# The router of batch 5 moved one or two places forward in the last batch of an attention loop

## The reference

```
# attention, per batch
q, k, v = x @ Wq.T, x @ Wk.T, x @ Wv.T
attn = softmax(q k / sqrt(D) + bias)
x = layernorm(x + (attn v) @ Wo.T)
# router
scores = sigmoid(xf @ gate_w.T)                  # [T, 32]
group_scores = scores.reshape(-1, 8, 4).max(-1)  # 8 groups
keep the 4 best groups; idx = top 6 experts of these
w = scores[idx] / sum * 2.5
# experts
y = sum over e of w[e] * (silu(xf @ w11[e].T) * (xf @ w33[e].T)) @ w22[e].T
shared = silu(xf @ sw1.T) * (xf @ sw3.T) @ sw2.T
x = layernorm(x + y + shared)
```

## Time and profile before

| | us |
|---|---|
| median of 3 runs | 552.78 |
| the three runs | 549.53, 552.78, 555.93 |
| the profiled execution | 551.69 |
| its span | 549.9 |
| PE busy | 463.3 (84%) |
| DVE busy | 367.0 (67%) |
| ACT busy | 320.9 (58%) |
| POOL busy | 226.6 (41%) |

### The profile page before, as it was taken

One profiled execution on the slowest core, in us unless ns is written; L12 is line 12 of the kernel. 1 busy time (PEld: TensorE's weight loads), 2 busy tenths in 40 slices (PEclk: granted clock), 3 DMA queues, 4 the chain that ended last, 5 costly groups with the idle time before them and its releaser, 6 DMA issues.

```text
span 549.9 us, 12959 instructions
## 1 busy us (share of the span) xinstructions
PE 463.3 (84%) x3218; PEld 385.7 (70%) x3219; DVE 367.0 (67%) x1711; ACT 320.9 (58%) x1087; POOL 226.6 (41%) x244
## 2 busy tenths in 40 slices
PE   4368878768878777879896999999999999999993
PEld 3245657556756555754356899999999999998772
DVE  4025586929696989787734677777777777771574
ACT  1049898848888898954103556555565555653024
POOL 0000000070435353737771557666666666665000
PEclk9757999979898999899998999999999999999998
DMA  4579749976959682439966855555555555521994
GB/s 133 120 232 253 176 113 259 238 225 202 237 138 237 179 202 71 142 95 401 413 233 188 307 160 166 151 156 167 147 166 151 165 165 165 153 73 66 421 414 171
DMA packets 68715, 107.92 MB, mean 196 GB/s; under 512 B 9269, under 2 KB 55098, under 8 KB 67520
## 3 DMA queue, kind: packets, MB, share of 16 engines
q1 hardware_dynamic: 53472, 74.62, 47.6%
q0 software_dynamic: 10752, 26.13, 14.3%
q10 hardware_dynamic: 4448, 6.65, 3.6%
HBM read 64.03 MB, written 43.33 MB: 195 GB/s over the span
## 4 chain that ended last, share of the span: by engine, by line
PE 45%; DMA 20%; DVE 10%; SPq 8%; POOL 6%; issue 6%; ACT 4%; POOLq 0%; ACTq 0%; DVEq 0%
PE bank L726 20%; PE bank L735 10%; POOL routed L1437 6%; DMA k_scratch<-k_lo 6%; DMA expert_w<-expert_out 6%; PE bank L716 5%; DVE s_neg L1015 4%; DMA k_pack<-k_scratch 4%; SPq L431 3%; ACT probs L831 2%; PE bank L500 2%; DMA xt<-xT 2%; SPq L382 2%; DMA xg_all<-routed 2%; PE bank L563 1%
## 5 line engine op out<-in xcount | busy, mean ns | idle before, releaser
L1437 POOL DMA_INDIRECT routed<-rows,position x96 | 93.5, 974 | 192.4 <-DVE position L1179 164.0
L1447 POOL DMA_INDIRECT expert_out<-rows,out_row x128 | 130.5, 1020 | 84.1 <-issue 61.2
L831 ACT ACTIVATE probs<-s_neg,m_neg 128x128 f32<-128x128 f32 (+1 forms) x256 | 113.9, 448 | 41.6 <-DVE m_neg L1015 41.4
L1015 DVE CUSTOM_DVE_ANT_0 s_neg<-bank,bias_sb 128x128 f32<-128x128 f32 (+1 forms) x256 | 79.8, 351 | 56.5 <-PE bank L532 55.3
L929 ACT ACTIVATE eg<-bank 128x128 f32<-128x128 f32 x128 | 35.5, 277 | 84.5 <-PE bank L726 82.5
L735 PE MATMUL bank<-expert_w,ea 128*128 x256 | 78.6, 389 | 2.2 <-issue 1.0
L532 PE MATMUL bank<-k_pack,q_pack 128*128 128x256 f32 (+1 forms) x128 | 59.3, 472 | 15.8 <-DMA k_pack<-k_scratch 13.2
L726 PEld LDWEIGHTS bank<-x1T,xn 128*128 128x128 f32 x512 | 67.9, 194 | 3.5 <-issue 0.3
L726 PE MATMUL bank<-x1T,xn 128*128 128x128 f32 x512 | 68.5, 277 | 0.0
L936 ACT ACTIVATE rows<-bank,pick 128x256 f32<-128x256 f32 x128 | 60.0, 468 | 2.6 <-DVE out_row L1346 2.2
L546 PE MATMUL bank<-cst,probs 128*128 128x128 f32 x256 | 44.2, 300 | 13.8 <-ACT probs L831 12.9
(11 more groups left out here) (162 smaller groups left out, 798.8 us busy)
## 6 DMA issues: line engine op xcount, KB each, us to landing
xg_all<-routed SPq DMA_DIRECT2D x128, 137.5 KB, 2.2
expert_w<-expert_out SPq DMA_DIRECT2D x16, 768.0 KB, 13.1
expert_w<-expert_weights SPq DMA_DIRECT2D x9, 1024.0 KB, 23.8
q_pack<-q_scratch SPq DMA_DIRECT2D x32, 256.0 KB, 4.7
routed<-empty SPq DMA_DIRECT2D x8, 550.0 KB, 13.5
k_pack<-k_scratch SPq DMA_DIRECT2D x16, 256.0 KB, 7.0
expert_w<-expert_weights ACTq DMA_DIRECT2D x8, 384.0 KB, 4.9
xt<-xT SPq DMA_DIRECT2D x9, 256.0 KB, 7.1
```

The costliest lines, as they stand in the source:

```text
L831: act.activation(probs[g % 2][qb][:, 2 * pair + r, :], s_neg[u][:, r, 0:n], ACT.Exp, bias=m_neg[:, u, r:r + 1], scale=-1.0, accum_out=row_ ...
L1015: dve.tensor_tensor_reduce(out=s_neg[u][:, r, 0:n], in0=SCORES[u][:, n * r:n * r + n], in1=bias_sb[:, REP * g + 2 * pair + r, SEQ - n:SEQ] ...
L1437: pool.indirect_dma_start(routed, bass.IndirectOffsetOnAxis(ap=position[b % ROW_BUFS][:, t, j:j + 1], axis=0), rows[b % ROW_BUFS][:, t, :] ...
L1447: pool.indirect_dma_start(expert_out, bass.IndirectOffsetOnAxis(ap=out_row[:, k:k + 1], axis=0), ey[k], None, bounds_check=TOKENS * TOPK - ...
```

## The change

In the last batch of the loop (`ahead` is false there and only there) the pieces of the router of batch 5 have a table of their own, `LAST_AT_UNIT`. Pieces 0, 1 and 2 keep their units, pieces 3 to 11 stand in an earlier unit than before. `ranks` of batch 5 stands on PE after unit (2, 1) instead of (3, 0).

```
-                        if g == 3 and u == 0 and two_behind:
+                        if (g, u) == ((3, 0) if ahead else (2, 1)) and two_behind:
                             ranks(b - 2, par)
...
             AT_UNIT = {(0, 1): (0,), (0, 2): (1,), (0, 3): (2,), (1, 1): (3,), (1, 2): (4, 5),
                        (1, 3): (6,), (2, 0): (7, 8), (2, 2): (9,), (3, 1): (10,), (3, 2): (11,)}
+            LAST_AT_UNIT = {(0, 1): (0,), (0, 2): (1,), (0, 3): (2, 3), (1, 1): (4, 5), (1, 2): (6,),
+                            (1, 3): (7, 8), (2, 0): (9,), (2, 2): (10,), (2, 3): (11,)}
...
-                            for piece in AT_UNIT.get((g, u), ()):
+                            for piece in (AT_UNIT if ahead else LAST_AT_UNIT).get((g, u), ()):
                                 router_piece(b - 2, par, piece)
```

## The result

The changed kernel takes 546.51 us (median of 16 runs, 541.82 to 551.98), the kernel before 549.0 us (median of 16 runs, 545.63 to 555.93). The ratio is 0.9939, with a 95% interval from 0.991 to 0.9969: a gain of 3.3 us, where 1.5 was forecast. The kernel before is faster here than in the three runs shown at first (552.78); this alone is 3.8 us. The profiled execution took 546.12 us, its span is 544.3.

What follows compares the result with a forecast made beforehand. POOL's 36 transfers, started by DVE's write of `position` of batch 5, were taken to bound the kernel. Savings of 0.59, 0.79 and 0.12 sum to 1.50 us: 552.78 - 1.5 = 551.3 us, range 547.9 to 554.6.

Steps and rivals of the forecast that it cites:

- What bounds the kernel: POOL's unbroken 36 transfers of batches 5 to 7, started by DVE's write of `position` of batch 5, release the slot loop.
- The three items: DVE work ahead of batch 5's `position` write: piece 3 -0.59, `norm` -0.79, piece 10 -0.12; sum -1.50 us.
- Piece 3 hidden: Router piece 3 moves into DVE's 0.95 us wait for a scores matmul in unit (0, 3): -0.59 us.
- `norm` behind the write: The own batch's `norm` on DVE now stands behind the write of `position` of batch 5: -0.79 us.
- all others only change places: DVE work between its scores wait and the `position` write, beyond three differing items, was claimed to add or save nothing.
- the fixed point: DVE's 0.95 us wait at 227.00 for a scores matmul, independent of the router, ahead of the moved pieces.
- No new wait: Last batch: PE's new wait of about 1.1 us at the ranks was to cost nothing, with 1.4 us of room.
- PE's wait at the ranks: PE waits about 1.1 us for piece 9 in the last batch; scores still reach DVE 1.4 us early.
- ACT's wait: ACT's 0.46 us wait for `bias_max` of unit (2, 0) grows by 0.73, absorbed by 0.81 of later waits.
- The margin of batch 6: Batch 6's positions were to be ready 0.86 us before POOL needs them, even if its router gains nothing.
- The first rival: TensorE's clock stays at 2.4 GHz at the slot loop's start, saving 0.8 us more: 550.5 us; chance 0.22.
- The second rival: PE's new wait at the ranks lowers the clock, delaying batch 6's positions; 1.0 us slower, 553.8 us; chance 0.06.

Runs made afterwards that it cites:

- late_ranks: Changed kernel with the ranks of batch 5 back in unit (3, 0) of PE, DVE keeping the new table; ratio to the kernel before 1.0004 (0.9978 to 1.003).
- warm_before: Kernel before with 8 more matmuls, results unused, on PE while it waits for the first slot's rows; ratio to the kernel before 0.9982 (0.996 to 1.0004).
- pool_late: Changed kernel with 10 small memsets on POOL ahead of the transfers of batch 5; ratio to the kernel before 0.998 (0.9957 to 1.0004).

## Why the prediction was right or wrong

**The level.** The forecast of 551.3 stands on a median of 552.78 from three runs. That was an unlucky draw: with 16 runs it is 549.0, and the 29 to 35 runs on each of the four chips used below give 547.3 to 548.1. On 549.0, by the sum, the changed kernel would have been at 547.5, still outside a range whose lower end was 547.9; the measured 546.51 lies 1.4 below that end. The step that failed is the range: it took the spread of three runs, 3.2 us to each side, around their own median, and not that this median itself could lie 3.8 us off. The same width around 547.5 would have held 546.51.

**What bounds the kernel** was right. The chain through POOL's 36 transfers stayed, and the slot loop follows the first of them at 51.02 to 51.20 us in all seven traces of the two kernels.

**The three items.** Piece 3 hidden: -0.59 forecast, 0.58 measured alone. `norm` behind the write: -0.79, 0.74 measured alone. Both: 1.38, and 1.38 measured. With piece 10 the sum is 1.50: 1.50 in one trace of the changed kernel and 1.43 in another, 1.24 and 1.21 in the two others. Most of the 0.26 that was missed is one slow DVE copy (below). It is no wait that the order adds, but "all others only change places" did not hold for it: L1034 took 0.50 to 0.53 us in 5 of the 11 traces with the new table, in which it stands 6.1 us behind the fixed point, and 0.29 in all 7 with the old places of pieces 4 to 11, in which it stands 4.8 to 5.4 behind it.

**No new wait.** PE's wait at the ranks (0.81 to 1.24 us), ACT's wait (1.04 to 1.41) and their absorption behind came as forecast. The margin of batch 6 was 1.01 us, where 0.86 was forecast; late_ranks shows what happens when it is used up, there with the help of a low clock.

**The first rival**, a clock that stays high at the slot loop, didn't come in any of four traces. PE's wait went from 4.3 to 5.0 down to 2.5 to 3.45 us, and the clock fell each time. What changed is when: in the last us before the first turn it was granted at 0.86, 0.50 and 0.50 in the three traces of the kernel before and at 1.00 in all four of the changed one, where it fell 0.5 to 1.7 us behind the turn. And the time from the first turn to the third slot is shorter in the mean (5.24 against 5.61). Its price was sized at 0.8; a clock that really stays high is worth 2.0. The forecast had left it out of the likeliest case altogether, where 0.4 of it belongs.

**The second rival**, a low clock that makes the router of batch 6 late, had no effect on the time of the changed kernel, but its first half is real. In two of the four traces the granted clock fell to 0.50 behind PE's new wait at the ranks, which it did in none of the seven traces that keep the ranks and pieces 4 to 11 in their old places. The positions of batch 6 came 15.29 and 15.38 us behind those of batch 5 instead of 14.99 and 15.00; that is within the 1.0 us that they had left, and the first transfers of a batch stayed 1.96 to 1.98 us behind the last of the one before. In late_ranks it did make POOL late, by 1.59 us. The Trainium skill ("TensorE: Matmul & The Clock Gate", section "A second HAM failure mode: psum-queue depth-cycling") says that short pauses between groups of matmuls can make the clock swing and cost throughput. The two falls, each behind one such pause, agree with it as far as they go, but they put no price on this change.

**What stays open.** Four comparisons of the changed kernel give 0.9918 to 0.9957; the stages give 0.9967. Three of the four intervals hold that value, one of them barely (their upper ends are 0.9969, 0.9982 and 0.9985); the fourth doesn't (0.9942). The mean of the four, 0.994, is 1.4 us more than the stages account for. In the traces the surplus lies in front of the fixed point, most of it where nothing differs between the kernels. Scatter there is shown (5.2 us between three traces of one kernel). And warm_before, with the old order, was 1.7 us faster than its stages too, which speaks against a further gain of the change itself. That scatter alone explains the surplus isn't shown; neither is another cause. The last run that was meant to decide it, pool_late, didn't.

## What to carry to other kernels

Where a string of equal work on one engine ends last, look for the single write that starts it, pick a wait of the writing engine in front of it as a fixed point, and list only what stands between the two in one order and not in the other: two small moves gave 1.38 of the 1.50 us that the write could gain. Cut every trace at such points: a stage that repeats to 0.01 us in one kernel and to 0.3 in the other can be judged by a few traces, where whole times scatter by 1%. Before a range is given, ask how far the starting level is known.

## What the runs showed of the hardware

**A DVE copy can slow down while POOL prepares a transfer.** The copy L1034 took 0.52 us in the first trace of the changed kernel and 0.29 in the second. The latter on DVE, then POOL in the same microsecond, then POOL in the first:

```profile
226.95 0.24 DVE L1031 RECIPROCAL l_inv<-row_sum 128x16 f32<-128x16 f32 x1
227.23 0.29 DVE L1034 COPY l_wide<-l_inv 128x256 f32<-128x256 f32 x1
```

```profile
226.17 0.97 POOL L1440 DMA_INDIRECT routed<-rows,position  x1 [0.30 <-issue]
227.45 0.97 POOL L1440 DMA_INDIRECT routed<-rows,position  x1 [0.30 <-issue]
```

```profile
228.06 0.97 POOL L1440 DMA_INDIRECT routed<-rows,position  x1 [0.30 <-issue]
```

In the second trace the copy (227.23 to 227.52) begins in the gap between two transfers (227.14 to 227.45); in the first (228.60 to 229.12) inside one (228.06 to 229.03). The median of this copy is 0.294 us in both kernels' traces, its longest 0.471 and 0.515. To lie inside a transfer isn't enough, though. In the third trace of the kernel before, it begins 0.33 us behind one's start and takes 0.29 (DVE, then POOL):

```profile
227.14 0.29 DVE L1034 COPY l_wide<-l_inv 128x256 f32<-128x256 f32 x1
```

```profile
226.81 0.98 POOL L1437 DMA_INDIRECT routed<-rows,position  x1 [0.30 <-issue]
```

Of the first such copy in the last batch there are 18, one in each trace. The five slow ones begin 0.54 to 0.56 us behind a transfer's start and end 1.06 to 1.07 behind it; the four that begin up to 0.40 behind it take 0.29, as in a gap. Why is not shown. The Trainium skill, "DMA: Bandwidth & Descriptors", section "SWDGE vs HWDGE vs iDMA", says that DVE in its two-port mode locks GpSimd out of the SBUF state in which it writes descriptors. No run here shows that direction; what they show is a longer copy on DVE.

**TensorE's clock can fall behind short waits, and their length alone doesn't decide.** At the slot loop it went to 1.2 GHz in the run with one added matmul, after waits of 0.61 and 0.78 us around it, and stayed at 2.4 GHz with 0.61 and 0.27, or 0.61 and none, all behind 5.5 us of dense work (L666); these are one or a few traces each. At the ranks it fell behind waits of 1.24 and 0.87 us, and not behind waits of 0.80 to 1.21 us in eight other traces. At the slot loop the low level cost 2.0 us in the mean, more than the edit gains in front of the write.
